# P times V in groups of three quarters behind every third softmax tile, in an attention and FP4 feed-forward layer

## What is computed

```python
qkv = (x @ w_qkv + b_qkv).reshape(b, n, 3, H, DH).transpose(2, 0, 3, 1, 4)
q, k, v = (qkv[0], qkv[1], qkv[2])          # then the rotary embedding on q and k
attn = jnp.einsum('bhqd,bhkd->bhqk', q, k) * scale
attn = jax.nn.softmax(attn, axis=-1)
out = jnp.einsum('bhqk,bhkd->bhqd', attn, v)
return out.transpose(0, 2, 1, 3).reshape(b, n, c) @ w_proj + b_proj
```

## Time and profile before

| | us |
|---|---|
| median of 3 runs | 3653.19 |
| lowest, highest | 3651.67, 3666.49 |
| the profiled execution's own time | 3661.47 |
| span of its instructions | 3659.7 |
| TensorE matmuls busy | 3412.5 |
| VectorE busy | 3367.8 |
| ScalarE busy | 2629.5 |

### The profile page before, as it was taken

The page is one execution under the profiler, slowest core; times in us unless marked ns, Lnnn a source line. Parts: engine busy times, 40 slices in busy tenths (PEclk is TensorE's granted clock), DMA queues, the critical chain, the costliest instruction groups (busy, mean ns, idle before and its releaser), DMA issues.

```text
span 3659.7 us, 69024 instructions
## 1 busy us (share of the span) xinstructions
PE 3412.5 (93%) x27752; PEld 1539.9 (42%) x27752; DVE 3367.8 (92%) x3565; ACT 2629.5 (72%) x4870; POOL 911.9 (25%) x995
## 2 busy tenths in 40 slices
PE   7668999999999999999999999999999969999997
PEld 4343333333333333333333333333333336666665
DVE  8898999999999989999999999999999739999997
ACT  4342888888888888888888888888888833333333
POOL 6881000010000000000000000000000028888887
PEclk9885999999999999999999999999999989999999
DMA  5442112221211111111111111111111111211110
GB/s 162 144 168 89 57 66 72 74 69 65 73 57 47 55 61 67 58 41 43 50 61 61 59 61 48 41 41 62 63 67 52 46 42 46 79 42 39 40 34 21
DMA packets 134508, 230.63 MB, mean 63 GB/s; under 512 B 29510, under 2 KB 84006, under 8 KB 121894
## 3 DMA queue, kind: packets, MB, share of 16 engines
q1 hardware_dynamic: 124972, 217.82, 17.6%
q10 hardware_dynamic: 9216, 8.39, 0.7%
HBM read 156.33 MB, written 68.16 MB: 61 GB/s over the span
## 4 chain that ended last, share of the span: by engine, by line
PE 81%; DVE 9%; ACT 3%; issue 3%; DMA 1%; POOL 1%; SPq 1%; ACTq 0%; POOLq 0%; DVEq 0%
PE ps L625 36%; PE ps L678 32%; PE ps L758 7%; PE ps L768 4%; DVE arena L980 2%; DVE arena L985 1%; PE ps L728 1%; ACT arena L842 1%; PE ps L665 1%; ACT arena L851 1%; DVE arena L973 1%; DVE arena L1003 1%; ACT arena L889 0%; DMA qst<-qk_parts 0%; ACT v_all L899 0%
## 5 line engine op out<-in xcount | busy, mean ns | idle before, releaser
L1003 DVE TENSOR_REDUCE arena<-ps 128x1 f32<-128x1024 f32 x2048 | 2495.0, 1222 | 120.8 <-PE ps L625 103.9
L851 ACT ACTIVATE arena<-ps 128x512 f32<-128x512 f32 x4096 | 2226.1, 597 | 364.6 <-PE ps L665 280.0
L625 PE MATMUL ps<-kst,qst 48*128 48x512 f32 x4096 | 1522.1, 452 | 26.5 <-DMA qst<-qk_parts 22.2
L665 PE MATMUL ps<-qst,kst 51*128 51x512 f32 x4096 | 1494.4, 448 | 0.0
L678 PE MATMUL ps<-arena 128*32 128x256 f32 x16384 | 1312.2, 393 | 71.1 <-ACT arena L842 67.2
L625 PEld LDWEIGHTS ps<-kst,qst 48*128 48x128 f32 x4096 | 615.4, 188 | 886.0 <-DVE arena L1003 716.2
L678 PEld LDWEIGHTS ps<-arena 128*32 128x32 f32 x16384 | 326.7, 108 | 797.5 <-issue 459.8
L1259 POOL TENSOR_TENSOR arena<-arena,ones 128x16 bf16<-128x16 f32 x64 | 14.2, 221 | 2432.6 <-DVE arena L1008 2432.6
L665 PEld LDWEIGHTS ps<-qst,kst 51*128 51x128 f32 x4096 | 606.6, 185 | 11.1 <-ACT arena L851 7.7
L768 PE MATMUL ps<-wdT,arena 128*128 128x256 f32 (+1 forms) x768 | 195.0, 407 | 48.5 <-ACT arena L889 46.2
L899 ACT ACTIVATE v_all<-ps 128x352 f32<-128x352 f32 x128 | 59.3, 463 | 239.1 <-PE ps L758 238.9
(11 more groups left out here) (104 smaller groups left out, 2223.9 us busy)
## 6 DMA issues: line engine op xcount, KB each, us to landing
qk_parts<-arena SPq DMA_DIRECT2D x32, 1024.0 KB, 7.4
kst<-qk_parts SPq DMA_DIRECT2D x128, 256.0 KB
qst<-qk_parts SPq DMA_DIRECT2D x128, 256.0 KB
kst<-qk_parts SPq DMA_DIRECT2D x128, 128.0 KB
qst<-qk_parts SPq DMA_DIRECT2D x128, 128.0 KB
att<-arena SPq DMA_DIRECT2D x256, 34.0 KB
arena<-in_xT SPq DMA_DIRECT2D x16, 512.0 KB, 8.2
arena<-in_x SPq DMA_DIRECT2D x32, 256.0 KB
```

The source lines that it names most:

```text
L625: mm = nc.tensor.matmul(ps[:, i % S_BANKS, :], q[SROW:SROW + STACK, qt * P:(qt + 1) * P], k[SROW:SROW + STACK, kc * CHUNK:(kc + 1) * CHUNK ...
L665: nc.tensor.matmul(ps[:, bank_of_t(g.c, i), :], kst[g.u % 2][first:first + ROWS, kb * P:(kb + 1) * P], qst[g.u % 2][first:first + ROWS, qb ...
L851: nc.scalar.activation(pt[kb % 2][:, qb * CHUNK:(qb + 1) * CHUNK], ps[:, bank_of_t(g.c, i), :], ACT.Exp).then_inc(p_ready, 1)
L1003: nc.vector.tensor_reduce(mx[g.u % 2][:, i // 2, i % 2:i % 2 + 1], ps[:, bank:bank + 2, :].rearrange("p b t -> p (b t)"), AX.X, ALU.max).t ...
```

## The change

- P times V is cut into quarters of 128 queries of each chunk (`QUARTERS`, `QUARTER`). A list made in advance (`products_behind`) says which quarters follow which T tile.
- They stand behind every third T tile, counted through all heads: after tiles 2, 5, 8 and so on. A slot takes three quarters, or four where seven or more are waiting (`MANY`), and never goes over the end of a head. Only key blocks whose last T tile lies at least two tiles back are taken (`TILES_BACK`).
- A slot may cross from one key block to the next. Quarters of one block in one slot are one matmul of up to 512 columns; where a slot crosses, there is one matmul for each block.
- There are three buffers of probabilities instead of two. The third lies in the arena at 28 * CHUNK words.
- The transpose of the maxima stands after tile 51, 52 or 53, whichever is the third of a run (`m_after`).
- `out_of_psum` follows the exponential of the tile behind which the last quarters of the head stand (`ENDS`), and the wait for a free buffer of probabilities goes by key blocks counted through all heads.
- In the last head whole key blocks follow each fourth tile, as before, as one group.

`AHEAD`, the S tiles, their banks and the order on VectorE stay as they are. In the repeating part of a head the slots hold three quarters of one block, or 1 + 2, or 2 + 1 quarters of two blocks; for the second head they stand after its tiles 1, 4, 7, 10, ..., 61, since 64 isn't a multiple of three.

```diff
@@ -70,9 +70,16 @@
 
 AHEAD = 20
 
-M_AFTER = 51
-
-HALF_AFTER = (1, 3)
+
+
+RUN, TILES_BACK = 3, 2
+QUARTERS, QUARTER = 4, 128
+
+MANY = 7
+
+P_BUFS = 3
+
+M_FROM = 51
 
 
 X_JOBS = B * N // CHUNK
@@ -140,14 +147,40 @@
                 fn(At(0, s - lag))
 
 
+def products_behind():
+
+    behind, done, head = {}, 0, KT * QUARTERS
+    for tile in range(G * TILES_S):
+        last_head = tile >= (G - 1) * TILES_S
+        if tile % RUN != RUN - 1 and not last_head or last_head and tile % CHUNKS != CHUNKS - 1:
+            continue
+        waiting = QUARTERS * max(0, (tile - TILES_BACK + 1) // CHUNKS) - done
+        count = waiting if last_head else min(waiting, QUARTERS if waiting >= MANY else QUARTERS - 1)
+        count = min(count, (done // head + 1) * head - done)
+        if count > 0:
+            behind[tile] = range(done, done + count)
+            done += count
+    return behind, range(done, G * head)
+
+
+BEHIND, AT_THE_END = products_behind()
+
+ENDS = {last.stop // (KT * QUARTERS) - 1: tile for tile, last in BEHIND.items() if last.stop % (KT * QUARTERS) == 0}
+
+
+def m_after(g):
+
+    return M_FROM + (RUN - 1 - g * TILES_S - M_FROM) % RUN
+
+
 def t_place(g, i):
 
-    return 1 + g * (TILES_S + 1) + i + (i > M_AFTER)
+    return 1 + g * (TILES_S + 1) + i + (i > m_after(g))
 
 
 def m_place(g):
 
-    return 0 if g == 0 else 1 + (g - 1) * (TILES_S + 1) + M_AFTER + 1
+    return 0 if g == 0 else 1 + (g - 1) * (TILES_S + 1) + m_after(g - 1) + 1
 
 
 def t_bank(place):
@@ -271,7 +304,8 @@
         take = carve(m_rows_start)
         m_rows = [take(P)[0:MROWS * KT] for _ in range(2)]
         take = carve()
-        pt = [take(N) for _ in range(2)]
+
+        pt = [take(N) for _ in range(P_BUFS - 1)] + [carve(12 * CHUNK + 16 * CHUNK)(N)]
         vs = [take(KT * 32, "p (t d) -> p t d", t=KT) for _ in range(2)]
         ost = [take(CHUNK) for _ in range(2)]
         sum_t = [take(KT) for _ in range(4)]
@@ -634,10 +668,10 @@
                 if back < 0:
                     return
                 g, i = divmod(back - 1, TILES_S + 1)
-                if back == 0 or i == M_AFTER + 1:
+                if back == 0 or i == m_after(g) + 1:
                     pe.wait_ge(mt_out, 1 if back == 0 else g + 2)
                 else:
-                    pe.wait_ge(p_ready, g * TILES_S + i - (i > M_AFTER) + 1)
+                    pe.wait_ge(p_ready, g * TILES_S + i - (i > m_after(g)) + 1)
 
             def m_tile(g):
 
@@ -666,20 +700,25 @@
                                  qst[g.u % 2][first:first + ROWS, qb * CHUNK:(qb + 1) * CHUNK],
                                  start=True, stop=True).then_inc(t_psum, 1)
 
-            def pv(g, kb, half):
-
-                if kb == 0 and half == 0:
-                    pe.wait_ge(v_staged, g.times(1, 1))
-                    wait_after(pe, o_out, g.times(1))
-                if half == 0:
-                    pe.wait_ge(p_ready, g.times(TILES_S, CHUNKS * (kb + 1)))
-                first = half * CHUNK // 2
-                for qb in range(CHUNKS):
-                    mm = nc.tensor.matmul(ps[32 * qb:32 * qb + 32, O_BANK, first:first + CHUNK // 2], vs[g.u % 2][:, kb, :],
-                                          pt[kb % 2][:, qb * CHUNK + first:qb * CHUNK + first + CHUNK // 2],
-                                          start=(kb == 0 and half == 0), stop=(kb == KT - 1 and half == 1))
-                if half:
-                    mm.then_inc(pv_step, 1)
+            def pv(quarters):
+
+                g, first = divmod(quarters.start, KT * QUARTERS)
+                if first == 0:
+                    pe.wait_ge(v_staged, g + 1)
+                    wait_after(pe, o_out, g)
+                pe.wait_ge(p_ready, CHUNKS * ((quarters.stop - 1) // QUARTERS + 1))
+                at = quarters.start
+                while at < quarters.stop:
+                    block, q = divmod(at, QUARTERS)
+                    n = min(quarters.stop - at, QUARTERS - q)
+                    cols = slice(q * QUARTER, (q + n) * QUARTER)
+                    for qb in range(CHUNKS):
+                        mm = nc.tensor.matmul(ps[32 * qb:32 * qb + 32, O_BANK, cols], vs[g % 2][:, block % KT, :],
+                                              pt[block % P_BUFS][:, qb * CHUNK + cols.start:qb * CHUNK + cols.stop],
+                                              start=(block % KT == 0 and q == 0), stop=(block % KT == KT - 1 and q + n == QUARTERS))
+                    at += n
+                    if q + n == QUARTERS:
+                        mm.then_inc(pv_step, 1)
 
             def head(g):
 
@@ -693,16 +732,10 @@
                         elif i >= TILES_S and not g.static(G - 1) and not g.static(G - 2):
                             s_tile(after, i - TILES_S)
                         t_tile(g, kb, qb)
-                        if kb * CHUNKS + qb == M_AFTER and not g.static(G - 1):
+                        if kb * CHUNKS + qb == m_after(g.c) and not g.static(G - 1):
                             m_tile(g.c + 1)
-                        halves = [HALF_AFTER.index(qb)] if qb in HALF_AFTER else []
-                        if g.static(G - 1):
-                            halves = [0, 1] if qb == CHUNKS - 1 else []
-                        for half in halves:
-                            if kb:
-                                pv(g, kb - 1, half)
-                            elif not g.static(0):
-                                pv(g.back(1), KT - 1, half)
+                        if g.c * TILES_S + kb * CHUNKS + qb in BEHIND:
+                            pv(BEHIND[g.c * TILES_S + kb * CHUNKS + qb])
 
             for i in range(TILES_S):
                 s_tile(At(0, 0), i)
@@ -714,8 +747,7 @@
             pe.wait_ge(v_out, 2 * NCH)
             pe.wait_ge(bias_done, 1)
             each_head(head)
-            for half in range(2):
-                pv(At(0, G - 1), KT - 1, half)
+            pv(AT_THE_END)
 
 
             pe.wait_ge(o_out, G)
@@ -844,15 +876,15 @@
             def head(g):
                 for kb in range(KT):
 
-                    wait_after(act, pv_step, g.times(KT, kb - 1))
+                    wait_after(act, pv_step, g.c * KT + kb - P_BUFS + 1)
                     for qb in range(CHUNKS):
                         i = kb * CHUNKS + qb
                         act.wait_ge(t_psum, g.times(TILES_S, i + 1))
-                        nc.scalar.activation(pt[kb % 2][:, qb * CHUNK:(qb + 1) * CHUNK],
+                        nc.scalar.activation(pt[(g.c * KT + kb) % P_BUFS][:, qb * CHUNK:(qb + 1) * CHUNK],
                                              ps[:, bank_of_t(g.c, i), :], ACT.Exp).then_inc(p_ready, 1)
-                        if not g.static(0) and kb == 1 and qb == 0:
+                        if not g.static(0) and g.c * TILES_S + i == ENDS[g.c - 1]:
                             out_of_psum(g.back(1))
-                        if i == M_AFTER and not g.static(G - 1):
+                        if i == m_after(g.c) and not g.static(G - 1):
                             maxima(g.c + 1)
 
             maxima(0)
```

## The result

The changed kernel takes **3882.99 us** (median of four runs, 3878.68 to 3884.37) against 3655.53 for the kernel before on the same chip: a ratio of **1.061** (95% interval 1.058 to 1.063). The forecast was 3879.

A forecast was written before the change was run, and what follows sets the result against it. TensorE was taken as the bound, VectorE 0.09 us behind. +3.7 us a head over 62.7 heads gave +230, less 4, on 3661.5: 3887.5, or 3879 us against the median; range 3755 to 3975.

The forecast's parts named there:

- What bounds: Steady part of the kernel before: TensorE sets the time at 1.233 us a pair, VectorE 0.09 us behind.
- The price of a group of three quarters: P times V on TensorE: 0.785 us from a three-quarter group's start to the next S tile.
- the upper bound of 1.05: Slots crossing a key block: at most 1.05 us, if no pass is shorter than 0.24 us.
- B's maximum: VectorE's maximum over the S pair with a product between its two tiles; forecast to start after 0.7 us idle.
- Fewer switches: Middle tile of three on TensorE falls from 0.34 to about 0.21 us; off the path, so no gain.
- The loop: Wait cycle through the S banks, with a product inside one pair: 4.16 us for six tiles against 3.70.
- VectorE's idle time: VectorE idles about 0.7 us before one maximum in three, some 670 times.
- The head's boundary: Between heads: the 1.1 us stall for the O_BANK copy goes, as the products are three tiles apart.
- The sum: Whole kernel: 44.5 us a head against 40.8, +230 us over 62.7 heads, less 4; 3879 us against the median.
- The faster one: Rival: the loop doesn't bind, fewer switches are all, VectorE is the bound; 3403 us, chance 9%.
- the point that decides: Price of the product inside the pair at which a head breaks even: 0.44 us, with gains below.
- The clock rival: Rival: TensorE's idle time lowers its clock; a tenth of the stage at 1.2 GHz gives 4004 us, chance 9%.

The follow-up runs named there:

- The halves by list: Changed kernel, but with two quarters behind every second tile as in the kernel before; three buffers and listed O_BANK copy kept: 3609.58 us, ratio 0.987.
- the groups behind tiles 3 and 5: Changed kernel with the group behind tile 2 of six moved behind tile 3, so every group follows a complete pair: 3745.63 us, ratio 1.024.
- The run with the pair kept whole: Changed kernel with the split pair's second S tile issued ahead of the group, its T tile running without an S tile: 3746.95 us, ratio 1.024.
- the mirror run: Changed kernel with products behind complete pairs cut to 16 columns in key blocks 1 to 14, those inside pairs whole: 4410.35 us.

## Why the prediction was right, step by step

- **What bounds.** TensorE before, with the S banks a slack of 0.4 us away. The halves by list (3609.58) show that the steady rhythm stays at 1.23 us a pair with all else changed. No run took work off TensorE in the old rhythm, so that TensorE sets the time there rests on the rows.
- **The price of a group of three quarters**, 0.785 worked out. The crossing one takes 1511.10 - 1510.31 = 0.79 in the fence above, so its four passes cost their columns, and the upper bound of 1.05 was never touched. For the whole one, 1508.75 - 1507.83 = 0.92 includes a wait of the S tile behind it for the end of B's maximum (1507.47 + 1.22), which the forecast covered only in general ("all else fits"). Where no such wait follows, as in the timeline of the groups behind tiles 3 and 5, the whole group takes 1848.07 - 1847.29 = 0.78.
- **Fewer switches.** The middle tile costs 1507.50 - 1507.27 = 0.23 (0.21 worked out). It is cheaper than a tile beside a product (0.33 or 0.34), as forecast, and gains nothing, since TensorE then waits.
- **The loop.** Worked out 4.16, measured 4.16: two maxima 2.36, 0.05 to the S tile, 0.43 to the product, 0.79, and 0.53 to the maximum. The order of S, product, S is binding because matmuls start in the order in which they are issued; the Trainium skill, TensorE: Matmul & The Clock Gate, in its part on packing small matmuls, says that they are never reordered among themselves, and the rows agree.
- **VectorE's idle time.** 0.7 us before each B was forecast, some 670 times. The table of waits has 411.3 us in 661 pieces, 0.62 each. The rest is a matter of counting: the forecast counts 1.14 for each of the three maxima of a cycle, but the last one's record is 1.22 long, and the idle time is counted from its end. That leaves 0.66.
- **TensorE's idle time** I put at 0.7 a cycle. From 1450 to 1491 us its matmuls are busy 36.37 of 41 us, 0.47 idle a cycle. The exposed weight loads lengthen the records of the matmuls (0.50 against 0.39) and probably take the rest.
- **The head's boundary.** The products' wait for the copy was 67.2 us in 63 pieces; in the changed kernel the copy (L874) ends one wait, of 0.6. In its place stand 67.6 us in 268 waits of products for exponentials, 0.25 each, in idle time, as the forecast had it (up to 0.3). The run with the pair kept whole probably brings such waits onto the path.

The changed kernel's table of waits from 370 to 3120 us: who waited for whom, us in total, times, longest.

```profile
DVE arena L1035 <- PE ps L659: 411.3, 661, 0.8
...
PE ps L659 <- DVE arena L1035: 196.7, 619, 0.4
PE ps L716 <- ACT arena L883: 67.6, 268, 0.3
```

- **The sum.** 44.5 us a head forecast, 44.43 measured (mean over the steady heads). Spans 3882.6 and 3659.7 differ by 222.9, forecast 226; the profiled execution of before had one stretch at the low clock that this one lacks.
- **Rivals.** The faster one needed an inside product below 0.44 us. Cutting it to 16 columns, 0.18 to 0.25 us to the next S tile in that run's trace, gives a kernel 2.4% faster than before; with two quarters, 0.57, it is 2.8% slower. So the point that decides lies between those two, which agrees with 0.44 and does not fix it. The clock rival did not occur, with 1.00 throughout the stage, but the mirror run shows that it was nearer than 9% may sound: it takes only less work behind the pairs.

What failed stood not in the forecast but in the experiments' expectations. That groups behind complete pairs would give 3530 to 3535 us failed at the step "T banks don't bind", true for a run of three. That work behind the pairs can go without a change of time failed at the clock. That the pair kept whole would take 3535 to 3630 us failed in part at the clock, and for the rest the cause is open.

## What to carry to other kernels

Where two engines hand tiles over through a few banks, look at what stands between the members of one hand-over, not only at how busy the engines are: 0.785 us of TensorE's work inside a pair made a cycle of 3.70 us one of 4.16, and the same work behind the pair was free while the clock was high. Count the banks of each side for the run length that a new order makes; here four S banks in pairs made products after an odd number of tiles dear, and three T banks made it dear to repeat runs of four (one such run in a head cost nothing). Together they left the old rhythm of two as the best one found among the kernels that do all the work. A change that bundles parts can hold a good one: the boundary's part alone is worth 1.3%.

## What the runs showed of the hardware

- Two maxima over 1024 columns in succession take 2.35 us where one alone takes 1.22; the spacing is 1.14, so with a busy share of 92% VectorE still had 0.09 us to spare in each pair.
- Cutting two fifths of P times V out of TensorE's idle time made the kernel 14% slower than the changed one (4410.35 against 3882.99): granted clock 0.69 over the stage against 1.00, and a cycle of 5.40 us against 4.16. Why the same cut in the other slots left it at 0.99 was not tested.
- Matmuls of 128 fp32 columns on a quarter of the array's columns, four beside each other, cost their columns: four passes of 128, 128, 256 and 256 columns take 0.79 us to the next tile, two of 384 columns 0.78.
